# A graph layer's edge sums: a block's sums loaded in 6 transfers of 4 runs instead of 3 of 12, attributes by 8 groups, 15 instead of 13 groups of rows on SyncE

## The chip, the cores and the metric

One core of a Trainium2 chip runs the kernel. The metric is the device time of one execution in microseconds (us), less is better. The median of three runs stands for a kernel.

## The reference

12500 nodes with 160 features each (64 scalars and 32 vectors of 3), 412500 edges sorted by their destination:

```python
h = relu(layernorm(x))
l0, l1 = h[:, :64] @ W_l1_0, h1 @ W_l1_1            # per node; h1: 32 vectors of 3
w = relu(edge_attr_10 @ W_fc1 * a) * b @ W_fc2      # per edge, 192 weights
y0, y1 = l0[src], l1[src]                           # a gather of 160 numbers per edge
m0, m1, m2, m3 = products of w, y0, y1, edge_attr_4 # per edge
s0..s3 = segment_sum(m0..m3, dst)                   # per node, 4 x 160 numbers
out = x + a_node * (h @ W_si + 0.5 * (s @ W_l2))    # per node
```

## The kernel before, in words

**Setup.** x is loaded by 14 pieces; per block of 128 nodes the layer norm's statistics, the transposes and the products with W_l1 are made, and the rows of l (160 numbers, 640 B) are written to the table T (`l_table`) in DRAM, four blocks at a time (L555). Meanwhile POOL gathers the raw x of 21 groups of edges, which SP stores in `raw_rows` (L547). ACT's queue loads the index tables: `bas` and `dsti` (1.6 MB each, into the space of R) in round q = 8 of 25, `src` (1.6 MB) in round 14. On DVE the function `test` compares them in pieces from round 11 on; its flag decides whether the main stage may run.

**Main stage.** The edges are 806 groups of 512 (4 tiles of 128). For each group PE makes the radial layer (L1189) and the 192 weights per edge (L1199), DVE multiplies them with the gathered rows (`weigh`, L1113 and L1116), PE sums a tile's products over windows of 8 nodes with a matrix of positions (`sums`, L1212), DVE moves the sums to E (L1100, 4 buffers), and SP stores E in DRAM as `s_tiles` (B), one store for two groups (L903).

The rows of l that a group needs come in four ways. POOL gathers them from T, four indirect DMAs per group, up to 6 groups ahead (L867). 21 groups are computed again from `raw_rows`. 13 groups (`ROW`, spread evenly by `single`) are fetched by SP, one DMA for each of 512 rows (L930), of an address in a register; 32 addresses are loaded into registers at a time (L927). 14 groups (`ROWA`) are fetched the same way by ACT (L1038). `rows_at(g)` deals out the 512 rows of a group evenly over the groups between its predecessor and itself, in SP's program order, so that some 8 or 9 rows stand behind each group's store.

For each of 98 blocks of 128 nodes, once the edges that may hold it are summed (`due`, every 8 or 9 groups), SP loads 512 rows of B with `load_tiles` (L646), 4 rows per partition, into Z; DVE makes the matrix D of which row belongs to which node; PE adds them up with D (`place`, L682), LATE = 2 groups and more after that; ACT, PE and DVE then transpose, multiply with `pw` and add x, and SP stores the block (L738). A row of B has 8 x 160 numbers: four sums of 160, of which `place` needs all of the first (s0 and s3's part) and slices of the three others. `pieces_of` cuts the first 160 in three overlapping runs of 54, so that a block is three DMAs with 12 runs per partition each: 216, 256 and 128 B. Z's row is three slots of 150 numbers.

The edge attributes `ea` are loaded by four groups (L878, [112, 512], two buffers), `e4` by twelve (L884). Whatever SP does stands in one queue: `store`, `load_tiles`, `load_ea`, `store_rows`, `rows_at`, in this order for each g. The last two blocks are loaded in chunks (`load_chunk`, L625).

Of the kernel before, what the change touches and what calls it, by code (L numbers as in the profile page):

```python
# [7 lines left out]
C = 160  # L8
# [5 lines left out]
NROW = 13  # L14
# [4 lines left out]
SLOT = 150  # L19
# [71 lines left out]
def build(nc, a, n_nodes, n_edges):  # L91
# [16 lines left out]
    ZW = C + 3 * SLOT  # L108
# [25 lines left out]
    with ctx:  # L134
# [52 lines left out]
        ea = sb("ea", [112, 2, GE])  # L187
# [3 lines left out]
        ZP = 3 * SLOT  # L191
# [287 lines left out]

        def test():  # L480

            V.wait_ge(s_b, 48)
# [4 lines left out]
            V.wait_ge(s_d, 16)  # L487
# [12 lines left out]
            link(V.tensor_scalar(vio[:, 5:6], vio[:, 0:1], float(WIN - 1), None, ALU.is_gt))  # L500
            V.scalar_tensor_tensor(vio[:, 8:9], vio[:, 6:7], 0.0, vio[:, 5:6], ALU.is_lt, ALU.add).then_inc(s_fl, 1)
            yield

        def main_weights():
# [6 lines left out]
            V.wait_ge(s_b, 48)  # L511
# [101 lines left out]
        def pieces_of(z, o, n):  # L613

            def rows(at, step, width):
                return bass.AP(tensor=B.tensor, offset=o + at, ap=[[8 * C, n], [step, 3], [1, width]])

            return ((z[:, :, 96:SLOT], rows(0, 53, SLOT - 96)), (z[:, :, 0:64], rows(3 * C, 2 * C, 64)),
                    (z[:, :, 64:96], rows(3 * C + 64, 2 * C + 32, 32)))

        def load_chunk(e, c, part):
            o = ((ends[L] - SPAN) * WIN + 128 * c) * 8 * C
            z = Z[:, L % 2, c, :].rearrange("p (k c) -> p k c", c=SLOT)
            to, of = pieces_of(z, o, 128)[part]
            e.dma_start(to, of).then_inc(s_zc[c], 16)  # L625
# [47 lines left out]
        def place(j, g):  # L673
# [3 lines left out]
            PE.wait_ge(s_z[j % 2], 48 * (j // 2 + 1))  # L677
# [127 lines left out]
        with nc.If(way == 0):  # L805
# [22 lines left out]
            s_rw = [sem(f"s_rw{i}") for i in range(len(ROW))]  # L828
            s_rwa = [sem(f"s_rwa{i}") for i in range(len(ROWA))]
# [84 lines left out]
            def row(i, n):  # L914
# [15 lines left out]
                SP.dma_start(lone[i % 2][p:p + 1, t, :].bitcast(u8), TB[:, bass.ds(v, 4 * C)]).then_inc(s_rw[i], 16)  # L930
# [19 lines left out]
            for g in range(NG):  # L950
# [8 lines left out]
                if g % 4 == 1:  # L959
                    load_ea(g // 4 + 2)  # L960
# [62 lines left out]
            def act_row(i, n):  # L1023
# [14 lines left out]
                AC.dma_start(lone_act[p:p + 1, i % 2, t, :].bitcast(u8), TB[:, bass.ds(v, 4 * C)]).then_inc(s_rwa[i], 16)  # L1038
# [111 lines left out]
            for g in range(NG):  # L1150
                V.wait_ge(s_wp, g + 1)
                for u in pairs(g):
# [27 lines left out]
            def radial(p):  # L1180
                if 2 * p >= NG:
                    return
                q = p // 2
                PE.wait_ge(s_ea[q % 2], 16 * (q // 2 + 1))
                for i in range(min(2, NG - 2 * p)):
# [3 lines left out]
                    m = PE.matmul(bank[i][0:100, 0:GE], w1s[o:o + 10, :], ea[o:o + 10, q % 2, :], start=True, stop=True)  # L1189
# [96 lines left out]
        with nc.Else():  # L1286
# [14 lines left out]
            row = sb("row", [128, 128], i32)  # L1301
            tri = sb("tri", [128, 128])
            sel = sb("sel", [128, 128])
            low = sb("low", [128, 128])
            one = sb("one", [128, 2], i32)
            ef = sb("ef", [128, 4])
            df = sb("df", [128, 3])
            ix = sb("ix", [128, 2, 4], i32)
# [7 lines left out]
            SP.dma_start(tri[:, :], a["tri"]).then_inc(f_0, 16)  # L1316
# [3 lines left out]
            with nc.Fori(0, NG * G) as i:  # L1320
# [13 lines left out]
                PE.matmul(bank[0][0:100, 0:128], w1s[0:10, :], ea[0:10, 0, 0:128], start=True, stop=True).then_inc(f_pe, 1)  # L1334
# [42 lines left out]
                for q in range(2):  # L1377
                    PE.matmul(bank[4 + q][:, 0:2 * C], sel[:, :], M[:, 2 * q:2 * q + 2, :], start=True,
# [19 lines left out]
def lay_out(v, n_nodes, n_edges):  # L1398
# [18 lines left out]
    NR = -(-NG // 4)  # L1417
# [34 lines left out]
    for d in range(3):  # L1452
        n = 53 if d < 2 else 54
        r = C + SLOT * d + 96
        pw[r:r + n] = zero[53 * d:53 * d + n]
# [71 lines left out]
```

## Time and profile before

| | |
|---|---|
| median of 3 runs | 3937.83 us (3935.28 to 3940.37) |
| the profiled execution | 3939.58 us, of it the span of the trace 3935.8 us |
| granted clock of TensorE | 0.863 of full speed |
| busy: PE, DVE, ACT, POOL | 83%, 60%, 19%, 75% of the span |
| DMA | 827774 packets, 589.86 MB |

The page's engines are PE (matrix products), DVE, ACT and POOL; SP (SyncE) has no arithmetic and is all queue. A "q" behind an engine's name marks its sequencer: an instruction that issues a DMA is busy there and not in the engine's busy time. In the timeline a row is one instruction, or several alike in a row (x8), with start and duration in us. The gather on POOL is an instruction of its own and does count as busy.

### The profile page before, as it was taken

How to read it: one execution, taken by the hardware profiler on the slowest of the kernel's cores; microseconds unless marked ns; L12 is line 12 of the kernel's file. 1: busy time of each engine (PE TensorE's matmuls, PEld its weight loads, DVE VectorE, ACT ScalarE, POOL GpSimd, SP SyncE). 2: the span in 40 equal slices, each digit the busy share in tenths (PEclk: the TensorE clock that was granted, in tenths of full speed). 3: DMA queues.
4: the chain of work that ended last, by engine and by line, in shares of the span. 5: the costliest groups of instructions: out<-in, count | busy, mean ns of one | idle time of the engine just before them, and what ended most of it. 6: DMA issues, size and time to landing. Idle time of an engine off the chain costs nothing.

```text
span 3935.8 us, 83918 instructions
## 1 busy us (share of the span) xinstructions
PE 3247.8 (83%) x17464; PEld 1918.8 (49%) x17464; DVE 2363.2 (60%) x8236; ACT 748.3 (19%) x1681; POOL 2947.5 (75%) x3119
## 2 busy tenths in 40 slices
PE   5788788888888877887888887988888888888887
PEld 4454444454444444444554444545454455555444
DVE  7455556565665656565666556556666566666655
ACT  5111112111111111111121212111112121211111
POOL 6777777777777777777777777777777777777776
PEclk8788889888998889788898889788888888989788
DMA  9565656565556565656566565656656565656655
GB/s 316 151 145 134 149 140 147 143 149 140 146 147 148 143 146 143 147 141 149 140 156 147 146 153 139 151 140 153 147 144 150 142 150 145 148 145 148 150 145 134
DMA packets 827774, 589.86 MB, mean 150 GB/s; under 512 B 535130, under 2 KB 748654, under 8 KB 826878
## 3 DMA queue, kind: packets, MB, share of 16 engines
q1 hardware_dynamic: 660752, 317.60, 31.0%
q0 software_dynamic: 149520, 255.42, 27.6%
q10 hardware_dynamic: 16990, 11.41, 1.1%
q8 instruction: 151, 2.47, 0.3%
q14 instruction: 361, 2.96, 0.2%
HBM read 429.06 MB, written 155.04 MB: 148 GB/s over the span
## 4 chain that ended last, share of the span: by engine, by line
PE 20%; SPq 18%; ACTq 16%; issue 15%; POOL 15%; DMA 10%; DVE 6%; ACT 2%; DVEq 0%; POOLq 0%
POOL R L867 13%; ACTq L1038 11%; SPq L930 10%; DMA R<-l_table,src 6%; PE bank L682 6%; PE bank L1199 6%; ACTq L1035 4%; PE bank L1212 3%; PE bank L1189 3%; DMA s_tiles<-E 3%; SPq L927 3%; DVE R L1116 3%; SPq L646 3%; PE bank L725 1%; DVE R L1113 1%
## 5 line engine op out<-in xcount | busy, mean ns | idle before, releaser
L867 POOL DMA_INDIRECT R<-l_table,src x3031 | 2865.7, 945 | 934.8 <-issue 843.3
L1199 PE MATMUL bank<-w,hs 100*128 100x192 f32 x6446 | 1388.0, 363 | 97.7 <-ACT hs L979 77.4
L1199 PEld LDWEIGHTS bank<-w,hs 100*128 100x128 f32 x6446 | 1181.3, 212 | 416.8 <-issue 286.0
L1113 DVE TENSOR_TENSOR R<-bank,R 128x256 f32<-128x256 f32 x1558 | 654.2, 420 | 1129.6 <-PE bank L1199 786.8
L1116 DVE TENSOR_TENSOR R<-bank,R 128x192 f32<-128x192 f32 x3116 | 954.2, 348 | 0.0
L1212 PE MATMUL bank<-R 128*32 128x320 f32 x6448 | 679.0, 495 | 307.1 <-DVE R L1116 300.3
L979 ACT ACTIVATE hs<-bank 100x512 f32<-100x512 f32 x806 | 437.4, 594 | 2159.1 <-PE bank L1189 991.3
L1100 DVE COPY E<-bank 128x320 f32<-128x320 f32 x806 | 391.8, 486 | 230.9 <-DMA s_tiles<-E 179.7
L1189 PE MATMUL bank<-ea,w1s 10*100 10x512 f32 x1612 | 515.0, 718 | 10.7 <-DMA ea<-in_ea_p 9.9
L682 PE MATMUL bank<-ZD 128*128 128x450 f32 x776 | 413.6, 688 | 100.2 <-issue 96.8
L1212 PEld LDWEIGHTS bank<-R 128*32 128x32 f32 x6448 | 143.8, 113 | 528.7 <-issue 411.7
L682 PEld LDWEIGHTS bank<-ZD 128*128 128x128 f32 x776 | 179.3, 243 | 349.9 <-issue 343.2
L1090 DVE TENSOR_TENSOR R<-bank,e 128x128 f32<-128x128 f32 x806 | 235.1, 292 | 27.4
L1189 PEld LDWEIGHTS bank<-ea,w1s 10*100 10x100 f32 x1612 | 113.2, 177 | 256.6 <-issue 245.4
L725 PE MATMUL bank<-pw,zt 128*128 128x160 f32 (+1 forms) x970 | 195.6, 359 | 49.2 <-ACT zt L719 44.2
L725 PEld LDWEIGHTS bank<-pw,zt 128*128 128x128 f32 (+1 forms) x970 | 167.9, 229 | 128.3 <-ACT zt L719 71.8
L1087 DVE TENSOR_TENSOR bank<-bank,rel 128x32 f32<-128x32 f32 x806 | 153.2, 190 | 0.0
L687 ACT ACTIVATE zz<-bank 128x450 f32<-128x450 f32 x98 | 53.6, 547 | 399.1 <-PE bank L682 380.4
L733 DVE SCALAR_TENSOR_TENSOR os<-bank,av,x 128x160 f32<-128x160 f32 x98 | 37.4, 382 | 117.4 <-PE bank L725 114.9
L296 POOL DMA_INDIRECT ZD<-in_xa,src_raw x84 | 81.7, 972 | 34.8 <-issue 25.0
L711 ACT ACTIVATE zt<-bank 128x512 f32<-128x512 f32 x97 | 58.1, 599 | 173.8 <-issue 114.6
L693 ACT ACTIVATE zz<-x,nb,rs 128x160 f32<-128x160 f32 x98 | 51.0, 521 | 137.0 <-issue 118.7
(114 smaller groups left out, 898.2 us busy)
## 6 DMA issues: line engine op xcount, KB each, us to landing
s_tiles<-E SPq DMA_DIRECT2D x395, 320.0 KB
lone_act<-l_table ACTq DMA_DIRECT2D x7168, 0.6 KB
psc<-l_table SPq DMA_DIRECT2D x3584, 0.6 KB
H<-l_table SPq DMA_DIRECT2D x3072, 0.6 KB
R<-l_table,src POOLq DMA_INDIRECT x3031
ea<-in_ea_p SPq DMA_DIRECT2D x202, 224.0 KB
ZD<-s_tiles SPq DMA_DIRECT2D x97, 384.0 KB
ZD<-s_tiles SPq DMA_DIRECT2D x97, 324.0 KB
```

What stands on the lines that cost most here:

```text
L682: m = PE.matmul(bank[7][:, 0:ZP], D[:, j % 2, c, :], Z[:, j % 2, c, :], start=c == 0, stop=c == NCH - 1)
L725: m = PE.matmul(home(j, placed)[:, 0:C], turned(j, placed, q)[0:n, :], pw[0:n, q, :], start=q == 0, stop=q == 4)
L867: PL.indirect_dma_start(out=Y[:, g % NB, t, :], out_offset=None, in_=T, in_offset=bass.IndirectOffsetOnAxis(ap=src[:, k:k + 1], axis=0),). ...
L930: SP.dma_start(lone[i % 2][p:p + 1, t, :].bitcast(u8), TB[:, bass.ds(v, 4 * C)]).then_inc(s_rw[i], 16)
L979: AC.activation(hs[:, g % 4, :], bank[g % 2][0:100, 0:GE], ACT.Relu, scale=REL).then_inc(s_hs, 1)
L1038: AC.dma_start(lone_act[p:p + 1, i % 2, t, :].bitcast(u8), TB[:, bass.ds(v, 4 * C)]).then_inc(s_rwa[i], 16)
L1100: V.tensor_copy(E[:, g % 4, :], bank[5 + g % 2][:, 0:2 * C]).then_inc(s_e, 1)
L1113: V.tensor_tensor(p[:, :, :, 0:64], w[:, :, 0:128].rearrange("p t (s c) -> p t s c", s=2), y[:, :, 0:64].unsqueeze(2).to_broadcast([128, n ...
L1116: m = V.tensor_tensor(p[:, :, s, 64:160].rearrange("p t (d c) -> p t d c", d=3), w[:, :, 128 + 32 * s:160 + 32 * s].unsqueeze(2).to_broadc ...
L1189: m = PE.matmul(bank[i][0:100, 0:GE], w1s[o:o + 10, :], ea[o:o + 10, q % 2, :], start=True, stop=True)
L1199: m = PE.matmul(b[:, o * 192:(o + 1) * 192], hs[:, g % 4, t * 128:(t + 1) * 128], w2[:, :], start=True, stop=True, skip_group_check=True)
L1212: m = PE.matmul(b[q, 0:2 * C], S[:, g % 2, t, :], P[:, g % 2, t, :], start=True, stop=True)
```

## The change

Three things are changed on SP and one in the setup.

A block's sums: the slots are 96 numbers instead of 150, and the first 160 numbers of a row are loaded whole, in a run of 640 B. The load is six DMAs with 4 runs per partition each (640, 384, 256, 128, 256, 128 B). The attributes are loaded by eight groups, with a layout in DRAM that keeps a partition's 4 KB together. SP fetches the rows of 15 groups instead of 13. The index tables are loaded in rounds 12, 14 and 18 instead of 8, 8 and 14, and the test's pieces run from round 15 on. The semaphores of the row buffers are shared by eight groups; the path of the flag that isn't taken uses D's space for its own tiles.

```diff
-NROW = 13
+NROW = 15
-SLOT = 150
+SLOT = 96
...
-    ZW = C + 3 * SLOT
+    ZW = 2 * C + 3 * SLOT
...
-        ea = sb("ea", [112, 2, GE])
+        ea = sb("ea", [112, 2, 2, GE])
...
-        ZP = 3 * SLOT
+        ZP = C + 3 * SLOT
...
+            if q == min(12, NQ - 1):
                 AC.dma_start(bas[:, :, :], a["bases"].rearrange("o (g t) -> o g t", t=G).to_broadcast([128, NG, G])
-                             ).then_inc(s_b, 16)
+                             ).then_inc(s_d, 16)
+            if q == min(14, NQ - 1):
                 AC.dma_start(dsti[:, :, :], a["dst_t"].rearrange("p (g t) -> p g t", t=G)).then_inc(s_d, 16)
-            if q == min(14, NQ - 1):
+            if q == min(18, NQ - 1):
                 AC.dma_start(src[:, :], a["src_t"]).then_inc(s_i, 16)
...
-            if q >= 11:
+            for _ in range(0 if q < 15 else 1 if q % 2 else 2):
                 next(pieces, None)
...
             r0 = (ends[j] - SPAN if ends[j] > SPAN else 0) * WIN
-            z = Z[:, j % 2, :, :].rearrange("p n (k c) -> p (n k) c", c=SLOT)
-            for to, of in pieces_of(z, r0 * 8 * C, 128 * NCH):
-                SP.dma_start(to, of).then_inc(s_z[j % 2], 16)
+            every = B[r0 * 8 * C:(r0 + 128 * NCH) * 8 * C].rearrange("(p c x) -> p c x", p=128, x=8 * C)
+            z = Z[:, j % 2, :, :]
+            SP.dma_start(z[:, :, 0:C], every[:, :, 0:C]).then_inc(s_z[j % 2], 16)
+            SP.dma_start(z[:, :, C:C + 96], every[:, :, 3 * C:3 * C + 96]).then_inc(s_z[j % 2], 16)
+            for k in (1, 2):
+                to, of = C + SLOT * k, (2 * k + 3) * C
+                SP.dma_start(z[:, :, to:to + 64], every[:, :, of:of + 64]).then_inc(s_z[j % 2], 16)
+                SP.dma_start(z[:, :, to + 64:to + 96], every[:, :, of + 64 + 32 * k:of + 96 + 32 * k]).then_inc(s_z[j % 2], 16)
...
-            PE.wait_ge(s_z[j % 2], 48 * (j // 2 + 1))
+            PE.wait_ge(s_z[j % 2], 96 * (j // 2 + 1))
...
-                if 4 * q >= NG:
+                if 8 * q >= NG:
                     return
                 if q >= 2:
-                    SP.wait_ge(s_h, 2 * q - 2)
-                SP.dma_start(ea[:, q % 2, :], a["ea_p"][q, :, :]).then_inc(s_ea[q % 2], 16)
+                    SP.wait_ge(s_h, 4 * q - 4)
+                SP.dma_start(ea[:, q % 2, :, :], a["ea_p"][:, 2 * q:2 * q + 2, :]).then_inc(s_ea[q % 2], 16)
...
-                if g % 4 == 1:
-                    load_ea(g // 4 + 2)
+                if g % 8 == 5:
+                    load_ea(g // 8 + 2)
```

## Rows read from the trace of the kernel before

**Rows 1.** The page: span, busy time of the engines, the chain that ended last.

```profile
span 3935.8 us, 83918 instructions
...
PE 3247.8 (83%) x17464; PEld 1918.8 (49%) x17464; DVE 2363.2 (60%) x8236; ACT 748.3 (19%) x1681; POOL 2947.5 (75%) x3119
...
PE 20%; SPq 18%; ACTq 16%; issue 15%; POOL 15%; DMA 10%; DVE 6%; ACT 2%; DVEq 0%; POOLq 0%
```

**Rows 2.** Waits of SP, 400 to 3700 us: us in total, times, longest.

```profile
SPq L903 <- DVE E L1100: 26.9, 42, 3.1
SPq L642 <- DMA s_tiles<-E: 15.4, 18, 2.4
SPq L927 <- DVE R L1116: 12.0, 8, 2.7
```

**Rows 3.** Groups of instructions, 400 to 3700 us: count, busy us, mean ns, idle before.

```profile
L867 POOL DMA_INDIRECT R<-l_table,src x2631 | 2487.5, 945 | 812.8 <-issue 731.7 <-DVE R L1116 81.1
...
L1100 DVE COPY E<-bank 128x320 f32<-128x320 f32 x702 | 341.4, 486 | 216.4 <-DMA s_tiles<-E 171.6 <-PE bank L1212 29.0 <-issue 0.8
```

**Rows 4.** SP's issues by line, 400 to 3700 us: ns minimum/median/maximum.

```profile
L930 SPq DMA_DIRECT2D H<-l_table x3072: 227/228/2052, 422.4 to 3551.7; - x192
...
L930 SPq DMA_DIRECT2D psc<-l_table x2854: 227/228/2185, 403.6 to 3699.7; - x191
...
L927 SPq TENSOR_LOAD <-src_row x185: 2037/2215/2849, 405.5 to 3677.9; - x185
...
L903 SPq DMA_DIRECT2D s_tiles<-E x352: 387/393/771, 408.8 to 3697.9; - x176
...
L646 SPq DMA_DIRECT2D ZD<-s_tiles x256: 595/877/4305, 399.2 to 3689.8; - x128
...
L878 SPq DMA_DIRECT2D ea<-in_ea_p x176: 334/458/1921, 409.3 to 3684.2; - x176
...
L738 SPq DMA_DIRECT2D out<-os x86: 377/468/2673, 401.0 to 3684.7; - x86
```

**Rows 5.** Timeline of SP, from 1053 us: start, duration, instruction.

```profile
1053.22 5.20 SPq L930 DMA_DIRECT2D H<-l_table  x16
1058.51 0.39 SPq L903 DMA_DIRECT2D s_tiles<-E  x1
1061.79 4.16 SPq L930 DMA_DIRECT2D H<-l_table  x13
```

**Rows 6.** Timeline of SP at two blocks' loads.

```profile
1035.81 3.39 SPq L646 DMA_DIRECT2D ZD<-s_tiles  x3
1039.31 3.71 SPq L930 DMA_DIRECT2D H<-l_table  x8
...
1071.35 4.59 SPq L646 DMA_DIRECT2D ZD<-s_tiles  x3
1076.05 3.92 SPq L930 DMA_DIRECT2D H<-l_table  x8
```

**Rows 7.** Timeline of SP in the setup, third and fourth load of x.

```profile
2.27 0.57 SPq L265 DMA_DIRECT2D x<-in_xp  x1
...
2.89 3.20 SPq L265 DMA_DIRECT2D x<-in_xp  x1
```

**Rows 8.** Issues of L555 and L625, whole span, and a timeline row of six.

```profile
L555 SPq DMA_DIRECT2D l_table<-ls x25: 372/373/2241, 22.9 to 107.6; - x25
...
L625 SPq DMA_DIRECT2D ZD<-s_tiles x11: 370/482/1791, 3899.6 to 3923.8; - x11
...
3899.61 4.45 SPq L625 DMA_DIRECT2D ZD<-s_tiles  x6
```

**Rows 9.** Timelines of ACT's queue, SP and POOL in the setup.

```profile
40.45 0.49 ACTq L471 DMA_DIRECT2D R<-in_bases  x1
...
40.91 13.40 SPq L547 DMA_DIRECT2D raw_rows<-ZD  x1
...
60.32 0.95 POOL L296 DMA_INDIRECT ZD<-in_xa,src_raw  x1 [7.10 <-DMA raw_rows<-ZD]
```

More of the change, by code:

```diff
@@ L480, in test @@
         def test():
-            V.wait_ge(s_b, 48)
+            V.wait_ge(s_b, 32)
             V.tensor_tensor(gap[:, 0, :], bound[:, 0, :], bound[:, 1, :], ALU.subtract)
@@ L486, in test @@
             yield
-            V.wait_ge(s_d, 16)
+            V.wait_ge(s_d, 32)
             for q in range(NCUT):
@@ L510, in main_weights @@
             V.tensor_scalar(src_act[:, :, :], src_act[:, :, :], 4.0 * C, None, ALU.mult).then_inc(s_by, 1)
-            V.wait_ge(s_b, 48)
+            V.wait_ge(s_b, 32)
             last = 1 if side_by_side(n_nodes, n_edges) else 0
@@ L611, in turned @@
             return zt[:, q, :]
[L613 to L619, printed above, removed]
         def load_chunk(e, c, part):
             o = ((ends[L] - SPAN) * WIN + 128 * c) * 8 * C
-            z = Z[:, L % 2, c, :].rearrange("p (k c) -> p k c", c=SLOT)
-            to, of = pieces_of(z, o, 128)[part]
-            e.dma_start(to, of).then_inc(s_zc[c], 16)
+            z = Z[:, L % 2, c, C:ZP].rearrange("p (k c) -> p k c", c=SLOT)
+            r = B[o:o + 128 * 8 * C].rearrange("(p k c) -> p k c", k=4, c=2 * C)
+            d = B[o + 3 * C + 64:o + 3 * C + 64 + 128 * 8 * C].rearrange("(p x) -> p x", x=8 * C)[:, 0:3 * (2 * C + 32)]
+            if part == 0:
+                e.dma_start(Z[:, L % 2, c, 0:C], r[:, 0, 0:C]).then_inc(s_zc[c], 16)
+            if part == 1:
+                e.dma_start(z[:, :, 0:64], r[:, 1:4, C:C + 64]).then_inc(s_zc[c], 16)
+            if part == 2:
+                e.dma_start(z[:, :, 64:96], d.rearrange("p (k c) -> p k c", k=3)[:, :, 0:32]).then_inc(s_zc[c], 16)
         def place_chunk(c):
@@ L652, in load_nodes @@
                 SP.wait_ge(s_t5, j - 1)
-            y = z[:, C:ZW].rearrange("p (k c) -> p k c", c=SLOT)
-            SP.dma_start(y[:, :, 96:SLOT], bass.AP(tensor=A.tensor, offset=j * 128 * 4 * C, ap=[[4 * C, 128], [53, 3], [1, 54]])
-                         ).then_inc(s_z[j % 2], 16)
+            y = z[:, 2 * C:ZW].rearrange("p (k c) -> p k c", c=SLOT)
+            SP.dma_start(z[:, C:2 * C], r[:, 0, :]).then_inc(s_z[j % 2], 16)
             SP.dma_start(y[:, :, 0:64], r[:, 1:4, 0:64]).then_inc(s_z[j % 2], 16)
@@ L827, in build @@
             s_rp = sem("s_rp")
-            s_rw = [sem(f"s_rw{i}") for i in range(len(ROW))]
-            s_rwa = [sem(f"s_rwa{i}") for i in range(len(ROWA))]
+            s_rw = [sem(f"s_rw{i}") for i in range(8)]
+            s_rwa = [sem(f"s_rwa{i}") for i in range(8)]
             lone = [psc[:, :, :].rearrange("p q c -> p (q c)")[:, 0:G * C].rearrange("p (t c) -> p t c", t=G),
@@ L929, in row @@
                 v = bass.RuntimeValue.of_register_unchecked(held_sp[n % RB]).with_bounds(min_val=0, max_val=(NP - 1) * 4 * C)
-                SP.dma_start(lone[i % 2][p:p + 1, t, :].bitcast(u8), TB[:, bass.ds(v, 4 * C)]).then_inc(s_rw[i], 16)
+                SP.dma_start(lone[i % 2][p:p + 1, t, :].bitcast(u8), TB[:, bass.ds(v, 4 * C)]).then_inc(s_rw[i % 8], 16)
                 SP.free_register(held_sp[n % RB])
@@ L1037, in act_row @@
                 v = bass.RuntimeValue.of_register_unchecked(held[n % RA]).with_bounds(min_val=0, max_val=(NP - 1) * 4 * C)
-                AC.dma_start(lone_act[p:p + 1, i % 2, t, :].bitcast(u8), TB[:, bass.ds(v, 4 * C)]).then_inc(s_rwa[i], 16)
+                AC.dma_start(lone_act[p:p + 1, i % 2, t, :].bitcast(u8), TB[:, bass.ds(v, 4 * C)]).then_inc(s_rwa[i % 8], 16)
                 AC.free_register(held[n % RA])
@@ L1162, in build @@
                     elif g in row_of:
-                        V.wait_ge(s_rw[row_of[g]], 16 * GE)
+                        V.wait_ge(s_rw[row_of[g] % 8], 16 * GE * (row_of[g] // 8 + 1))
                     elif g in rowa_of:
-                        V.wait_ge(s_rwa[rowa_of[g]], 16 * GE)
+                        V.wait_ge(s_rwa[rowa_of[g] % 8], 16 * GE * (rowa_of[g] // 8 + 1))
                     else:
@@ L1182, in radial @@
                     return
-                q = p // 2
+                q, h = p // 4, p // 2 % 2
                 PE.wait_ge(s_ea[q % 2], 16 * (q // 2 + 1))
@@ L1188, in radial @@
                     o = 64 * (p % 2) + 32 * i
-                    m = PE.matmul(bank[i][0:100, 0:GE], w1s[o:o + 10, :], ea[o:o + 10, q % 2, :], start=True, stop=True)
+                    m = PE.matmul(bank[i][0:100, 0:GE], w1s[o:o + 10, :], ea[o:o + 10, q % 2, h, :], start=True, stop=True)
                 m.then_inc(s_h, 1)
@@ L1300, in build @@
             BIG = float(1 << 22)
[L1301 to L1308, printed above, removed]
+            row = D[:, 0, 0, :].bitcast(i32)
+            tri = D[:, 0, 1, :]
+            sel = D[:, 0, 2, :]
+            low = D[:, 0, 3, :]
+            one = D[:, 1, 0, 0:2].bitcast(i32)
+            ef = D[:, 1, 1, 0:4]
+            df = D[:, 1, 2, 0:3]
+            ix = D[:, 1, 3, 0:8].bitcast(i32).rearrange("p (b k) -> p b k", b=2)
             M = Y[:, 1, 0:4, :]
@@ L1315, in build @@
                          flat_zt[:, 0:4 * C].unsqueeze(1).to_broadcast([128, NT, 4 * C])).then_inc(f_0, 16)
-            SP.dma_start(tri[:, :], a["tri"]).then_inc(f_0, 16)
+            SP.dma_start(tri, a["tri"]).then_inc(f_0, 16)
             for e in (PL, V):
@@ L1324, in build @@
                 four = nc.snap(i * 64 + 64, min_val=64, max_val=NG * G * 64)
-                SP.dma_start(ea[0:10, 0, 0:128], a["ea_t"][:, bass.ds(e0, 128)]).then_inc(f_ld, 16)
+                SP.dma_start(ea[0:10, 0, 0, 0:128], a["ea_t"][:, bass.ds(e0, 128)]).then_inc(f_ld, 16)
                 SP.dma_start(one[:, 0:1], a["src_f"][bass.ds(e0, 128), :]).then_inc(f_ld, 16)
                 SP.dma_start(one[:, 1:2], a["dst_f"][bass.ds(e0, 128), :]).then_inc(f_ld, 16)
-                SP.dma_start(row[:, :], a["dst_r"][:, bass.ds(e0, 128)].to_broadcast([128, 128])).then_inc(f_ld, 16)
-                SP.dma_start(ef[:, :], a["e4_f"][bass.ds(e0, 128), :]).then_inc(f_ld, 16)
+                SP.dma_start(row, a["dst_r"][:, bass.ds(e0, 128)].to_broadcast([128, 128])).then_inc(f_ld, 16)
+                SP.dma_start(ef, a["e4_f"][bass.ds(e0, 128), :]).then_inc(f_ld, 16)
                 for e in (PE, PL, V):
@@ L1333, in build @@
                                       in_offset=bass.IndirectOffsetOnAxis(ap=one[:, 0:1], axis=0)).then_inc(f_g, 16)
-                PE.matmul(bank[0][0:100, 0:128], w1s[0:10, :], ea[0:10, 0, 0:128], start=True, stop=True).then_inc(f_pe, 1)
+                PE.matmul(bank[0][0:100, 0:128], w1s[0:10, :], ea[0:10, 0, 0, 0:128], start=True, stop=True).then_inc(f_pe, 1)
                 AC.wait_ge(f_pe, 1)
@@ L1347, in build @@
                 flink(V.tensor_copy(df[:, 0:1], one[:, 1:2]))
-                flink(V.tensor_scalar(sel[:, :], row[:, :], df[:, 0:1], None, ALU.is_equal))
-                flink(V.tensor_tensor(low[:, :], sel[:, :], tri[:, :], ALU.mult))
-                flink(V.tensor_reduce(df[:, 1:2], low[:, :], AX.X, ALU.max))
+                flink(V.tensor_scalar(sel, row, df[:, 0:1], None, ALU.is_equal))
+                flink(V.tensor_tensor(low, sel, tri, ALU.mult))
+                flink(V.tensor_reduce(df[:, 1:2], low, AX.X, ALU.max))
                 flink(V.tensor_scalar(df[:, 2:3], df[:, 1:2], BIG, None, ALU.mult))
@@ L1377, in build @@
                 for q in range(2):
-                    PE.matmul(bank[4 + q][:, 0:2 * C], sel[:, :], M[:, 2 * q:2 * q + 2, :], start=True,
+                    PE.matmul(bank[4 + q][:, 0:2 * C], sel, M[:, 2 * q:2 * q + 2, :], start=True,
                               stop=True).then_inc(f_pe, 1)
@@ L1416, in lay_out @@
     w1s = np.zeros((112, 100), f)
-    NR = -(-NG // 4)
+    NR = -(-NG // 8) * 2
     both = np.zeros((10, NR * 4 * GE), f)
@@ L1420, in lay_out @@
     both = both.reshape(10, NR, 4, GE).transpose(1, 2, 0, 3)
-    ea_p = np.zeros((NR, 112, GE), f)
+    ea_p = np.zeros((112, NR, GE), f)
     for r in range(4):
         w1s[32 * r:32 * r + 10] = v["L0_gnn_W_fc1"]
-        ea_p[:, 32 * r:32 * r + 10] = both[:, r]
+        ea_p[32 * r:32 * r + 10] = both[:, r].transpose(1, 0, 2)
     one = np.zeros((C, C), f)
@@ L1441, in lay_out @@
     pw[0:64, 0:64] = v["L0_gnn_W_si0"]
-    zero = np.zeros((C, C), f)
-    zero[0:64, 0:64] = v["L0_gnn_W_l2_00"]
+    pw[160:224, 0:64] = v["L0_gnn_W_l2_00"]
     for d in range(3):
@@ L1446, in lay_out @@
         pw[64 + 32 * d:96 + 32 * d, q] = v["L0_gnn_W_si1"]
-        zero[q, q] = v["L0_gnn_W_l2_11"]
-        r = C + SLOT * d
+        pw[224 + 32 * d:256 + 32 * d, q] = v["L0_gnn_W_l2_11"]
+        r = 2 * C + SLOT * d
         pw[r:r + 64, q] = v["L0_gnn_W_l2_01"]
@@ L1451, in lay_out @@
         psc[r + 64:r + 96] = k / np.sqrt(3.0)
[L1452 to L1455, printed above, removed]
     fold = lambda m: np.ascontiguousarray(m.reshape(5, 128, C).transpose(1, 0, 2))
```

## The prediction

> **What bounds the kernel now.** The first part of the page [rows 1] shows PE busy for 83% of the span, POOL for 75%, DVE for 60%, and its chain of waits divides itself between PE, SyncE's queue (18%), ACT's queue and POOL: no engine stands out, so busy shares don't answer the question. I take the steady part of the main stage, 400 to 3700 us, and ask each sequence of instructions how long it stood still.
>
> In that stretch DVE evacuated 702 groups [rows 3], so a group takes 3300 / 702 = 4.70 us. POOL made 2631 gathers of 945 ns, with 812.8 us between them, of which 731.7 us is issue time (about 0.305 us each) [rows 3]. 2631 x 1.25 us = 3289 us of 3300: POOL never rests. The reader is to see there that a busy share of 75% is a full engine. What takes 4 gathers away from POOL is worth 4 x 1.25 = 5.0 us, if nothing else is full.
>
> But SyncE (SP) is full too. It waited 26.9 + 15.4 + 12.0 us in the three largest rows [rows 2]; with the smaller ones I take 60 us. It works for 3240 of 3300 us, 98%. This can be added up from counts [rows 4] and prices. A row issue of L930: 16 in 5.20 us and 13 in 4.16 us [rows 5], the last one counted with its 0.23 us alone, is 0.33 us each with the register move; the load of 32 addresses (L927) is 2.2 us by its median [rows 4] and 0.09 us of gaps, 2.3 us. A store of E is 0.39 + 0.05 us, a load of attributes 0.46 + 0.05, an output store 0.47 + 0.05. So: 5926 rows x 0.33 = 1956; 185 loads x 2.3 = 426; 352 stores x 0.44 = 155; 176 x 0.51 = 90; 86 x 0.52 = 45.
>
> The last item is the block's sums (L646), and its price is larger than its own rows say. Three issues take 3.39 us in one block and 4.59 us in another, and what follows is late as well: the 8 rows behind them take 3.71 and 3.92 us [rows 6], where 7 x 0.33 + 0.23 = 2.54 us is usual. With 0.1 us of gap the two blocks cost 4.66 and 6.07 us; I take 5.4 us. 85 blocks x 5.4 = 459 us. The sum is 3131 us of the 3240, the rest (109 us) being the loads of e4 and of raw rows and small irregularities. The budget closes within 4%, and SP has next to nothing to give.
>
> **The change part by part.**
>
> Rows: two more groups are fetched by SP, 1024 rows. 1024 x 0.33 + 32 x 2.3 = +412 us of SP. POOL loses 8 gathers, 8 x 1.25 = -10 us. No DVE, PE or ACT instruction is added; a weighing from the row buffer costs what one from Y costs. The groups stand 52 to 55 apart instead of 58 to 64, and the first one at 52 instead of 60, so its 512 rows go out in 46 groups.
>
> Attributes: half as many issues of the same 112 partitions, each twice as long. 101 x 0.51 = -52 us of SP. They are asked for two buffers ahead, so that a longer landing is hidden behind at least 6 groups (28 us).
>
> A block's sums: 36 runs per partition in 3 issues become 24 runs in 6, 4608 runs against 3072 for the 128 partitions; bytes are nearly the same (7200 and 7168 per partition). Why does the present load cost 5.4 us? The first issue of 1536 runs takes about 0.6 us (its minimum in [rows 4] is 595 ns), and the maximum there is 4305 ns: something fills up and the queue holds SP back. The loads of x in the setup give its size from another side: each is 896 runs; the third was taken in 0.57 us and the fourth took 3.20 us [rows 7]. So 2688 runs are taken without a stall, and 3584 are not. The new load has 3072 in all, spread over six issues' time, in which the first ones drain. Without a stall an issue of 512 runs is that of L555, 373 ns [rows 8], and for one right behind another the chunk loads of L625 (384 runs) have a median of 482 ns [rows 8]. 0.39 + 5 x 0.48 + 6 x 0.05 = 3.1 us. Call the cost of a block X. The bounds: from below, six at L555's price with gaps, 2.5 us; from above, the stall stays whole, 5.4 us. The nearest row is the run of six L625 issues in 4.45 us [rows 8], one of which stalled (1791 ns at most). I take 3.1, because one stall in eleven such issues is rare. The 94 blocks that are loaded while rows are being issued save 94 x (5.4 - 3.1) = -216 us.
>
> The cheapest issue of the trace, a row's single run of 640 B, takes 227 ns, and the store of E takes at least 387 [rows 4]. The Trainium skill (DMA: Bandwidth & Descriptors, "Anatomy of one DMA") puts the sequencer's dispatch of a DMA at about 50 ns and calls descriptor generation small. The trace does not agree; an estimate by that page would be 0.3 us for six issues, and SP would have room to spare.
>
> The layout: the product of a block is 448 columns instead of 450, the last transpose 96 rows instead of 98: nothing. The weights' rows are moved with it. The loads are wanted only from LATE on (two groups and more), so that six landings are as good as three.
>
> The setup: `bas`, `dsti` and `src` go out one at a time and later. In the trace the first two are issued at 40.4 us back to back, SP's next store of raw rows then takes 13.40 us, and POOL stands for 7.10 us, its only long wait before the main stage [rows 9]. POOL runs from there into the main stage without a pause. If the three loads fit between others the 7 us go; each is still 1.6 MB, so I take -6 us, with 0 and -7 as ends. The pieces of the test on DVE are dealt out over later rounds and end in the last one, as before.
>
> **The sum.** SP: +412 - 52 - 216 = +144 us of work. SP's present idle time (60 us in 3300, some 65 in the whole stage) absorbs what it can; the waits for a landed store (15.4 us, [rows 2]) stay, so about 55 can be used. That leaves +89 us. SP takes the place of POOL as the engine that sets the pace. Whoever is late next: the store of E waits in SP's queue behind rows, DVE waits for its buffer (already 171.6 us of L1100's idle time [rows 3]), then PE for DVE, and POOL for its Y buffers. POOL's 10 us are lost in it. With the setup's -6: +83 us. The profiled execution took 3939.6 us (3935.8 of span and 3.8 around it), which is 1.8 us above the median of the runs; 3939.6 + 83 = 4023, less 1.8 and with the tail after the last row untouched: 4020 us. In general the time is about 3729 + 94 X.
>
> **The rivals.**
>
> SP becomes the bound and the stall goes (the forecast): X from 2.5 to 4.45 us gives 3964 to 4147. For it: the 98% and the additive budget. Against: the budget has 109 us that I can't name. Chance 0.56.
>
> The stall stays: the DMA engines drain the runs at their own pace, and six issues wait for it as three did. X = 4.45 to 5.4 and over, 4147 to 4237. For it: the row behind the three issues is late too, so what fills up is not emptied by pausing; the present blocks cost 4.7 to 6.1 us. Against: the x loads' 2688 runs. Chance 0.24. The Trainium skill (the same page, "Specifications") says that below 512 B a transfer is short of line rate; of the 24 new runs only 4 are longer, so by it the engines' time falls little, which speaks for this rival. The two blocks of [rows 6] can't tell that from a limit on the number of runs.
>
> The other side: POOL stays the bound. It decides at X = 2.1 us: 3729 + 94 x 2.1 = 3926, which is where POOL's own time lies, 3938 - 10 - 6 = 3922. Faster by 0.4%. For it: the row issues could lose part of their unexplained 109 us once the queue is no longer choked, worth another 1 us of X; then 2.5 to 3 would do. Or an issue of 512 runs costs only what a row's issue does, 0.23 us [rows 4]: then X is 6 x 0.23 + 0.3 = 1.7 us, 3729 + 160 = 3889, and POOL's 3922 decides. The page's rule on dispatch, weighed above, would lead to this as well. Against: 512 runs took 372 ns at the least [rows 8], so that six are 2.5 us, and a trade of 412 us against 268 can't come out even. Chance 0.14 (0.02 of it for the cheap issue). Between this case and the forecast, X of 2.1 to 2.3 us, the time stays within 0.2% of now: 0.06.
>
> **How the numbers follow.** A measurement of this kernel tells 0.2% (8 us) from no change. Faster 0.14, within 0.2% 0.06, slower 0.80. The time is the first case's, 4020, with its own range 3964 to 4147. The range for 8 in 10 reaches down to POOL's case at 3924 and up to 4150, into the case of the stall that stays; some 0.06 is left out below and 0.14 above.
>
> **What would show it.** In the profile after: group time of about 4.8 us in the steady stretch; SP's waits for DVE (L903) near zero; POOL's idle time released by DVE no longer 81 us but several tens of us more; DVE's idle time at L1100 by the landing of the store of E well over 171.6 us; the issues of a block near 0.4 to 0.5 us each with no issue over 2 us, and the 8 rows behind them in 2.5 us; no POOL wait of 7 us in the setup. The prediction is wrong if POOL's gathers still follow one another every 1.25 us, which would mean that a row or a block costs SP less than these rows say.

## The result: slower by 6%, SyncE sets the pace

The changed kernel took 4178.3 us in the median of 4 runs (4173 to 4184), the kernel before 3936.6 us beside it: ratio 1.061 (95% interval 1.059 to 1.064). The forecast was 4020 us, with a range up to 4150. The direction and the mechanism are as forecast; the loss is 242 us where 82 were forecast, nearly three times as much.

The page of the changed kernel, its span, its engines and the chain that ended last:

```profile
span 4180.0 us, 86178 instructions
PE 3314.1 (79%) x17464; PEld 1956.0 (47%) x17464; DVE 2357.8 (56%) x8236; ACT 746.8 (18%) x1681; POOL 2939.8 (70%) x3111
...
SPq 53%; issue 15%; PE 12%; DMA 7%; ACTq 7%; DVE 4%; POOL 1%; ACT 1%; DVEq 0%; POOLq 0%
SPq L934 32%; SPq L931 9%; ACTq L1042 5%; DMA s_tiles<-E 5%; PE bank L1203 3%; PE bank L686 3%; SPq L651 3%; SPq L650 2%; SPq L907 2%; PE bank L1216 2%; PE bank L1193 2%; ACTq L1039 2%; DVE R L1120 1%; SPq L647 1%; SPq L742 1%
```

SP's queue had 18% of the chain in [rows 1] and has 53% now; its rows (L934) and the loads of their addresses (L931) alone make 41%. The reader is to see also what doesn't show it: the busy shares of PE, DVE, ACT and POOL have all fallen by 1 to 5 points, since all wait, and SP has no busy share at all.

Who waited for whom, SP's own waits and two groups of DVE and POOL, 400 to 3900 us of the changed kernel (as [rows 2, 3], in a stretch 200 us longer):

```profile
SPq L642 <- DMA s_tiles<-E: 20.5, 19, 2.7
...
SPq L907 <- DVE E L1104: 5.0, 18, 0.4
SPq L931 <- DVE R L1120: 4.9, 6, 1.3
```

```profile
L1104 DVE COPY E<-bank 128x320 f32<-128x320 f32 x696 | 339.9, 488 | 486.8 <-DMA s_tiles<-E 424.3 <-PE bank L1216 39.2 <-issue 5.7
...
L871 POOL DMA_INDIRECT R<-l_table,src x2606 | 2463.6, 945 | 1036.7 <-issue 698.3 <-DVE R L1120 338.4
```

A group takes 3500 / 696 = 5.03 us instead of 4.70. SP waits for DVE's sums 5.0 us in all where it waited 26.9 [rows 2]. DVE waits 424.3 us for the store of E where it waited 171.6, and POOL 338.4 us for the Y buffers where it was 81.1 [rows 3]: the chain of followers that the prediction named.

A block's load in the timeline of SP, changed kernel, two blocks (as [rows 6]):

```profile
1007.36 0.53 SPq L646 DMA_DIRECT2D ZD<-s_tiles  x1
1007.94 0.62 SPq L647 DMA_DIRECT2D ZD<-s_tiles  x1
1008.62 0.66 SPq L650 DMA_DIRECT2D ZD<-s_tiles  x1
1009.32 0.64 SPq L651 DMA_DIRECT2D ZD<-s_tiles  x1
1010.00 0.63 SPq L650 DMA_DIRECT2D ZD<-s_tiles  x1
1010.67 1.47 SPq L651 DMA_DIRECT2D ZD<-s_tiles  x1
1012.24 5.66 SPq L934 DMA_DIRECT2D H<-l_table  x10
...
1049.95 0.53 SPq L646 DMA_DIRECT2D ZD<-s_tiles  x1
...
1053.34 0.66 SPq L651 DMA_DIRECT2D ZD<-s_tiles  x1
1054.10 3.32 SPq L934 DMA_DIRECT2D H<-l_table  x10
```

From the first issue to the first row 4.88 and 4.15 us; the ten rows behind are 0.1 to 0.2 us over their usual time (9 x 0.33 + 0.23 = 3.2, and 2.3 for the register load that the first ten contain). So these two blocks cost SP 5.0 and 4.3 us. Read in the same way, all 85 blocks between 400 and 3900 us take 4.77 us on average from the first issue to the next instruction, and what follows is 0.3 us late: 5.1 us a block. The forecast had 3.1. The last issue took over 1 us in 47 of the 85. The 85 blocks of the kernel before, 400 to 3700 us, cost 5.7 us (4.39 and 1.3) where the prediction took 5.4 from two of them. The issues of these lines over the whole span, ns minimum/median/maximum:

```profile
L650 SPq DMA_DIRECT2D ZD<-s_tiles x194: 518/649/2089, 209.6 to 4158.8; - x194
...
L651 SPq DMA_DIRECT2D ZD<-s_tiles x194: 518/677/1922, 210.2 to 4159.4; - x194
```

**A measure for SP.** What a kernel asks of SP is the stretch less SP's waits, by group. It is 4.61 us before (3300 less the 62 us of all its waits, 702 groups) and 4.97 for the changed kernel (3500 less 39.6, 696 groups). POOL needs 4.67 to 4.69, its gathers per group in the stretch at 1.25 us each. SP's number is used below. A stall at an issue is counted in it as work, and it comes from one execution of each kernel.

### The profile page after: what moved, and what is told of

Same layout as the page of the kernel before. It is cut to its first block, busy times and chain, and to the rows that moved or that the text cites. A ratio compares the mean times of both kernels' runs of the same rounds, so it can differ in the third digit from the quotient of the medians.

```text
span 4180.0 us, 86178 instructions
## 1 busy us (share of the span) xinstructions
PE 3314.1 (79%) x17464; PEld 1956.0 (47%) x17464; DVE 2357.8 (56%) x8236; ACT 746.8 (18%) x1681; POOL 2939.8 (70%) x3111
## 4 chain that ended last, share of the span: by engine, by line
SPq 53%; issue 15%; PE 12%; DMA 7%; ACTq 7%; DVE 4%; POOL 1%; ACT 1%; DVEq 0%; POOLq 0%
SPq L934 32%; SPq L931 9%; ACTq L1042 5%; DMA s_tiles<-E 5%; PE bank L1203 3%; PE bank L686 3%; SPq L651 3%; SPq L650 2%; SPq L907 2%; PE bank L1216 2%; PE bank L1193 2%; ACTq L1039 2%; DVE R L1120 1%; SPq L647 1%; SPq L742 1%
## 5 line engine op out<-in xcount | busy, mean ns | idle before, releaser
L1203 PEld LDWEIGHTS bank<-w,hs 100*128 100x128 f32 x6446 | 1203.3, 215 | 416.4 <-issue 283.1
L686 PE MATMUL bank<-ZD 128*128 128x448 f32 x776 | 459.3, 754 | 232.9 <-issue 219.7
L1193 PE MATMUL bank<-ea,w1s 10*100 10x512 f32 x1612 | 524.1, 730 | 14.0 <-DMA ea<-in_ea_p 13.2
L686 PEld LDWEIGHTS bank<-ZD 128*128 128x128 f32 x776 | 199.4, 270 | 507.1 <-issue 488.6
L729 PE MATMUL bank<-pw,zt 128*128 128x160 f32 (+1 forms) x970 | 186.7, 348 | 51.0 <-ACT zt L723 45.9
L691 ACT ACTIVATE zz<-bank 128x448 f32<-128x448 f32 x98 | 53.2, 543 | 594.1 <-PE bank L686 584.2
L709 PEld LDWEIGHTS bank<-ident,zz 128*128 128x128 f32 x392 | 44.4, 149 | 69.9 <-issue 69.0
```

Source lines behind the costliest of these rows:

```text
L686: m = PE.matmul(bank[7][:, 0:ZP], D[:, j % 2, c, :], Z[:, j % 2, c, :], start=c == 0, stop=c == NCH - 1)
L729: m = PE.matmul(home(j, placed)[:, 0:C], turned(j, placed, q)[0:n, :], pw[0:n, q, :], start=q == 0, stop=q == 4)
L1203: m = PE.matmul(b[:, o * 192:(o + 1) * 192], hs[:, g % 4, t * 128:(t + 1) * 128], w2[:, :], start=True, stop=True, skip_group_check=True)
```

## The experiments

Of 18 runs, 6 (f and i, on two chips) were beside a kernel before of 3936 or 3937 us. The 12 others (e, g, h, j) ran on three other chips, where the kernel before took 5526 to 5613 us at a granted clock near 0.71; the last section has what is known of that. Their ratios are given, but the arithmetic of the prediction is tried on f and i.

| run | groups of rows | a block's load | before there, us | ratio (95%) | SP's work per group, us |
|---|---|---|---|---|---|
| changed | 15 | 6 close together | 3936.6 | 1.061 (1.059 to 1.064) | 4.97 |
| f1 | 13 | 6 close together | 3936.2 | 0.998 (0.997 to 0.999) | 4.46 |
| f2 | 15 | 3 close together, all else as before | 3936.2 | 1.084 (1.082 to 1.086) | 5.09 |
| f3 | 15 | 6, both sides of one shape | 3936.2 | 1.057 (1.055 to 1.059) | 4.95 |
| f4 | 15 | 6 between rows | 3936.2 | 1.056 (1.054 to 1.057) | 4.90 |
| i1 | 15 | 3 between rows | 3936.7 | 1.053 (1.051 to 1.055) | 4.89 |
| i2 | 14 | 3 between rows | 3936.7 | 1.020 (1.016 to 1.023) | 4.67 |
| e1 | 13 | as f1 | 5606.9 | 0.994 (0.991 to 0.998) | |
| e2 | 15 | as f2 | 5606.9 | 1.047 (1.043 to 1.051) | |
| e3 | 13 | 6, attributes and index tables loaded as before | 5606.9 | 0.998 (0.997 to 1.000) | |
| e4 | 15 | as f3 | 5606.9 | 1.031 (1.027 to 1.035) | |
| g1, h1 | 15 | as i1 | 5525.8, 5530.4 | 1.037, 1.038 (each within 0.004) | |
| g3, h2 | 14 | as i2 | 5525.8, 5530.4 | 1.013, 1.014 (each within 0.004) | |
| g4, h3, j1 | 15 | 3 of the 6 | 5525.8, 5530.4, 5613.4 | 1.019, 1.021, 1.019 | |
| j2 | 14 | 6 close together | 5613.4 | 1.015 (1.011 to 1.019) | |

**Rows alone: e1, f1, e2, f2, e3.** Theory A: SP's queue is the bound and the rows filled it. Its rival B: the six loads land late and hold the sums up.

```diff
-NROW = 15
+NROW = 13
```

> The changed kernel with the rows of 13 groups on SP instead of 15; six loads, attributes by eight groups and the later index tables stay. Theory A (SP's queue sets the pace; the two groups of rows are what it can't carry): 1024 rows x 0.41 us = 418 us of work leave SP, which then needs about 3762 us where POOL needs 3930, so POOL's gathers set the pace again: 3925 to 3945 us, ratio 0.997 to 1.002. Theory B (the six loads of a block land later or hold the matrix sums up, and the rows are harmless): little changes, above 4100 us.

> The same kernel as e1_rows13 once more, because there the kernel before itself took 5607 us with a granted clock of 0.70. Theory A: POOL's gathers follow one another every 1.25 us, 3925 to 3945 us where the kernel before takes 3938. Theory B: above 4100.

f1 took 3927.3 us, 9 us less than before; in e1 the ratio was 0.994. With the same six loads and 13 groups nothing is slow, so B falls. f2 is the kernel before with `NROW = 15` alone:

> The kernel before with the rows of 15 groups on SP and nothing else of the change. Theory A: 3938 + 418 of row work - 50 of SP's idle time that is used up = 4300 us (4270 to 4330), slower than the changed kernel's 4178 by what six loads and the attributes save. Theory B: the rows cost nothing, 3925 to 3945 us.

> The same kernel as e2_before_rows15 once more, where the kernel before takes 3938. Theory A: 4270 to 4330 us. Theory B: 3925 to 3945.

4267.4 us: the rows alone cost 331 us, and the time is 3 us under the expected range. The rest of the change gives back 89 of them. e3 has the six loads with 13 groups, and of the rest of the change only the shared semaphores, the flag's other path and the attributes' layout in DRAM:

> The kernel before with a block's sums in six loads (and the layout that belongs to them), 13 groups of rows, attributes by four groups, index tables where they were. Theory A: SP gets freer by 50 to 70 us of work and POOL sets the pace as before: 3930 to 3945 us. Theory B: above 4100 us.

0.998 (0.997 to 1.000), on a slower chip only: no measurable cost, and hardly a gain. f1's groups and SP's largest waits, 400 to 3700 us (as [rows 2, 3]):

```profile
L871 POOL DMA_INDIRECT R<-l_table,src x2638 | 2493.9, 945 | 807.2 <-issue 738.1 <-DVE R L1120 69.1
...
L1104 DVE COPY E<-bank 128x320 f32<-128x320 f32 x704 | 341.3, 485 | 90.9 <-DMA s_tiles<-E 55.6 <-PE bank L1216 22.9 <-issue 1.4
```

```profile
SPq L907 <- DVE E L1104: 105.3, 65, 6.5
SPq L642 <- DMA s_tiles<-E: 23.1, 22, 2.6
SPq L931 <- DVE R L1120: 15.9, 10, 2.6
```

POOL makes 2638 gathers in 3300 us, one per 1.251 us, and SP waits 160.7 us in all (105.3 of them for DVE). What the change frees on SP is what SP now stands idle: POOL can't use it.

**An issue's price by its shapes: e4, f3.** In the changed kernel the DRAM side of a transfer is 512 rows with one stride and the SBUF side 128 partitions of 4. With another assignment of rows both sides are (128, 4, width). A partition then takes rows 128 apart instead of 4 neighbours, so that the order of the addresses changes with the shapes.

```diff
-... .rearrange("(p c x) -> p c x", p=128, x=8 * C)
+... .rearrange("(c p x) -> p c x", p=128, x=8 * C)
```

> The changed kernel, but partition p of a block's load takes rows p, 128 + p, 256 + p, 384 + p of the sums instead of rows 4p to 4p + 3, so that both sides of each transfer have the same three dimensions (128, 4, width); the matrix of positions follows. Runs, bytes and issues are the same. Theory P (an issue's price depends on the shapes: 0.65 us now against 0.48 us for the chunk loads, whose two sides match): six issues get cheaper by about 1 us, 94 blocks, about 4085 us. Theory Q (an issue behind another costs 0.65 us and the last one waits for room whatever the shapes): 4170 to 4190 us.

> The same kernel as e4_mapped once more. In e4_mapped an issue of a block's load had medians of 0.39 us for the first and 0.50 for the others, against 0.53 and 0.63 in e1_rows13. Six issues are then 0.75 us cheaper, 94 blocks, 70 us of SP: 4178 - 70 = 4110 us (4090 to 4125). If SP's queue weren't the bound, or if room in the queue and not the issue set the price, it would stay at 4170 to 4190.

f3 took 4159.7 us, 19 us less than the changed kernel's 4178.3, where 70 were expected. Its timeline shows why:

```profile
1003.52 1.43 SPq L650 DMA_DIRECT2D ZD<-s_tiles  x1
1004.99 1.63 SPq L651 DMA_DIRECT2D ZD<-s_tiles  x1
...
1044.61 0.40 SPq L646 DMA_DIRECT2D ZD<-s_tiles  x1
1045.06 0.55 SPq L647 DMA_DIRECT2D ZD<-s_tiles  x1
1045.66 0.49 SPq L650 DMA_DIRECT2D ZD<-s_tiles  x1
1046.19 0.51 SPq L651 DMA_DIRECT2D ZD<-s_tiles  x1
1046.74 0.51 SPq L650 DMA_DIRECT2D ZD<-s_tiles  x1
1047.30 0.92 SPq L651 DMA_DIRECT2D ZD<-s_tiles  x1
1048.32 3.23 SPq L934 DMA_DIRECT2D H<-l_table  x10
```

The first four issues are each 0.1 to 0.2 us cheaper than in the changed kernel's blocks, as theory P has it, and the last ones take much of it back: 0.92 us here, 1.43 and 1.63 in the block before. Over all 85 blocks between 400 and 3900 us the last issue took more than 1 us in 68, where it was 47 of 85 in the changed kernel, and a block costs 4.9 us instead of 5.1; 94 x 0.2 = 19 us is what the time fell by. Issues that come faster stall more often at the end. P holds for the price and fails for the time.

**Issues apart from one another: f4.** One issue, then one after every second row of the same group.

```diff
+                            if n % 2 == 0:
+                                load_part()
```

> The changed kernel with the six issues of a block's load put between the rows of the same group (one, then one after every second row) instead of one behind another. Runs, bytes and order are the same. Theory Q (an issue close behind another large one costs more, 0.65 against 0.53, and the last ones and the next instruction wait for room, 1.1 us a block): 5 x 0.12 + 1.1 = 1.7 us a block, 94 blocks, 4178 - 160 = 4020 us (3990 to 4060). Theory P (the price belongs to the shapes and the stalls to the number of runs, wherever they stand): 4160 to 4190.

f4 took 4151.2 us, 27 us less where 160 were expected. Its timeline of SP:

```profile
1083.94 0.52 SPq L658 DMA_DIRECT2D ZD<-s_tiles  x1
1084.57 0.74 SPq L941 DMA_DIRECT2D H<-l_table  x2
1085.36 0.52 SPq L658 DMA_DIRECT2D ZD<-s_tiles  x1
1085.98 0.43 SPq L941 DMA_DIRECT2D H<-l_table  x1
1086.46 0.52 SPq L658 DMA_DIRECT2D ZD<-s_tiles  x1
1087.08 0.57 SPq L914 DMA_DIRECT2D s_tiles<-E  x1
```

An issue takes 0.52 us, and the stalls are gone: the longest of 582 took 0.96 us. But whatever stands behind one is dearer: a row 0.43 instead of 0.23 us, two rows 0.74 instead of 0.56, a store of E 0.57 instead of 0.39; over the stretch of 400 to 3900 us it is 0.19 us on average. An issue of 512 runs costs 0.52 + 0.1 + 0.2 = 0.8 us in its place, six of them 4.9. The sum for Q had counted the stall and forgotten this.

**Three issues between rows: g1, h1, i1; with 14 groups: g3, h2, i2.** After f4 theory S was a price per issue, and its rival D the time in which the DMA engines drain the runs. The old load of three issues is put between the rows:

```diff
+                            if m % 4 == 0:
+                                load_part()
```

> The changed kernel with the old load of a block (three issues of 12 runs per partition, slots of 150 numbers), these three put between the rows of the same group (one, then one after every fourth row); 15 groups of rows, attributes by eight groups, later index tables. Theory S (what a block costs SP is a price per issue: in f4_spread each of six took 0.53 us, 0.08 of gaps and 0.19 more in the row behind it; three of 0.60 + 0.08 + 0.19 are 2.6 us against 5.1): 4178 - 94 x 2.5 = 3943 us (3925 to 3970). Theory D (the queue gives room no faster than the DMA engines drain the runs, about 5 us a block, so that what is saved in one place comes back in another, as in f3_mapped and f4_spread): with 4608 instead of 3072 runs no better than 4150, up to 4230.

> The same kernel as g1_three_spread15 once more, because there the kernel before took 5526 us with a granted clock of 0.71 and each row of SP cost 0.56 us where it costs 0.35 otherwise. In g1 an issue between rows had medians of 0.60, 0.59 and 0.57 us and the row behind it took 0.49 on average (0.26 more than usual): 3 x (0.59 + 0.08 + 0.26) = 2.8 us a block against 5.1. Theory S, where the kernel before takes 3938: 4178 - 94 x 2.3 = 3962 us (3945 to 3980). Theory D: 4150 to 4230.

> The kernel of g1 and h1 a third time, for a chip on which the kernel before takes 3938. Theory S: 3962 us (3945 to 3980). Theory D: 4150 to 4230.

i1 took 4148.0 us, 2 us under D's range. S is refuted: half the issues bring 3 us against f4, which is within the spread of the executions. D isn't shown by it: 4608 runs took no longer than f4's 3072. SP's timeline in i1, with issues of 1536 runs:

```profile
1007.36 0.59 SPq L655 DMA_DIRECT2D ZD<-s_tiles  x1
1008.05 2.07 SPq L939 DMA_DIRECT2D H<-l_table  x4
1010.17 0.59 SPq L655 DMA_DIRECT2D ZD<-s_tiles  x1
1010.85 1.94 SPq L939 DMA_DIRECT2D H<-l_table  x2
...
1046.76 0.59 SPq L655 DMA_DIRECT2D ZD<-s_tiles  x1
1047.44 1.63 SPq L939 DMA_DIRECT2D H<-l_table  x4
1049.12 0.59 SPq L655 DMA_DIRECT2D ZD<-s_tiles  x1
1049.80 1.15 SPq L939 DMA_DIRECT2D H<-l_table  x2
```

The issues are 0.59 us, and the rows behind them take 2.07, 1.94, 1.63 and 1.15 us where four take 1.22 and two 0.56: 0.85, 1.38, 0.41 and 0.59 us more, 0.8 on average. Over the stretch of 400 to 3900 us it is also 0.8. An issue of 1536 runs costs 0.59 + 0.1 + 0.8 = 1.5 us, three of them 4.5. Three issues more and 1536 runs less are worth about the same to SP here, which is why a load of six could not pay for 1024 rows.

> g1_three_spread15 with 14 groups of rows. Theory S: SP has 208 us less than in g1, so POOL sets the pace, with four gathers fewer than in f1_rows13: 3927 - 5 = 3922 us (3915 to 3930), faster than both kernels. Theory D: 3940 to 4020.

> The same kernel as g3_three_spread14 once more, where the kernel before takes 3938. Theory S: SP needs 3962 - 208 = 3754 us and POOL sets the pace: 3922 us (3915 to 3930). Theory D: 3940 to 4020.

> The kernel of g3 and h2 a third time, for a chip on which the kernel before takes 3938. Theory S: 3922 us (3915 to 3930). Theory D: 3940 to 4020.

i2 took 4015.4 us, in D's range. Its SP needs 4.67 us per group and POOL as much, but the pace was 3500 / 729 = 4.80, and SP waited 95 us of that stretch. The chain that ended last in i2 is PE 30%, ACT's queue 24%, SP's queue 13% and POOL 2%: neither SP nor POOL alone held it, and what PE and ACT's queue had to do with it was not tried.

**Half of the load left out: g4, h3, j1, and 14 groups as they are: j2.** g4, h3 and j1 leave three of a block's six issues out, so that parts of the sums aren't computed.

> The changed kernel without three of the six issues of a block's load (the last three: the second vector part's 32, the third's 64 and 32 numbers); their columns of the sums hold what an earlier block left, so that this part of the output isn't computed. 1536 instead of 3072 runs, still one behind another. Theory S: three issues at about 0.8 us less, 94 x 2.4 = 226: 3950 us (3935 to 3970). Theory D: the engines' time for the runs falls from 4.2 to 2.5 us by the packets' mean durations, 1.7 us a block: 4178 - 160 = 4018 (3990 to 4040).

> The same kernel as g4_three_of_six once more (three of the six issues of a block's load left out), where the kernel before takes 3938. Theory S: 3950 us (3935 to 3970). Theory D: 4018 us (3990 to 4040).

> The kernel of g4 and h3 (three of the six issues of a block's load left out, 1536 runs, one behind another; that part of the sums isn't computed) once more, for a chip on which the kernel before takes 3937. Theory M, formed after i1 and f4: on SP a large issue costs 0.42 us and 0.75 ns for each run, the instruction behind it included (512 runs: 0.53 + 0.08 + 0.19 = 0.80 us in f4; 1536 runs: 0.60 + 0.07 + 0.90 = 1.57 us in i1). Three issues of 512 runs less save 3 x 0.8 = 2.4 us or a little more with the stall of the last one, 94 x 2.5 = 235: 3943 us (3930 to 3965). Theory D (drain alone): 4018 (3990 to 4040).

> The changed kernel with 14 groups of rows on SP, nothing else different. SP's work is linear in the rows: 4178 - 512 x 0.41 = 3968 us if SP alone sets the time (3955 to 3985). If two queues that are both almost full cost extra, as i2 seems to show (SP waited 102 us there, and the time was 75 us over SP's line), 4000 to 4060. If POOL alone set it, 3922.

All four ran on the slower chips. There the load of half the runs is 0.9 to 1.2% under e4 (whose load has the other shapes; the changed kernel itself has no run there), and 14 groups are 1.5% over the kernel before where 13 are 0.6% under it. The order is that of theory A, but none of the numbers decides between M (a price for each issue and each run, in j1's expectation) and D, and the excess of i2 has no second measurement.

## Why the prediction was wrong

- *What bounds the kernel* was right. POOL without a pause and SP at 98% is what f1 and f2 confirm: two groups of rows on a queue with 60 us to spare cost 331 us.
- *Rows, +412 us of SP.* Between f1 and the changed kernel SP's work rises from 4.459 to 4.972 us per group, 806 x 0.513 = 413 us. Between the kernel before and f2 it is 4.613 to 5.087, 806 x 0.474 = 382 us.
- *A block's sums: the step that failed is the cost X of the six issues, "I take 3.1".* It measured 5.1 over the 85 blocks, and the old load 5.7 where 5.4 was taken, so that a block saves 0.6 us and not 2.3: 94 x 0.62 = 58 us of SP instead of 216. SP's work says the same. Before to f1, all of the change but the rows saves 806 x (4.613 - 4.459) = 124 us; less the 52 taken for the attributes 72 us are left, 0.8 per block; from f2 to the changed kernel it is 806 x (5.087 - 4.972) - 52 = 41 us, 0.4 per block. With 58 in the place of 216 the prediction's own sum gives 4020 + 158 = 4178 us, the measured time. That it hits so closely is luck: SP's waits were to give 55 us and gave 25 (806 x (62 / 702 - 39.6 / 696)), and other terms must have made up for that.
- Three things were wrong inside X. The 0.48 us of L625 come from transfers whose two sides have the same shape; here the shapes differ and the second to sixth issues have medians of 0.62 to 0.68 us (f3 brought them to 0.50 to 0.58). The loads of x were read as proof that 3072 runs find room; the last issue took over 1 us in 47 of 85 blocks. And nothing was set down for the instruction behind an issue, which f4 and i1 show to be 0.2 us late after 512 runs and 0.8 after 1536. The nearest row for six issues was in the prediction, 4.45 us [rows 8], and was argued away as a rare stall.
- *The rival "the stall stays"* described the time better (4147 to 4237) and named the reason only in part: f4 removed the stalls, and SP's work fell by 0.07 us per group, 57 us, the time by 27.
- *The rival that POOL stays the bound* fell: POOL's gathers came every 1.34 us and not every 1.25 (3500 / 2606). The reason given against it sets 412 us against 268; at the 2.5 us for six issues that it speaks of, the saving would be 94 x 2.9 + 52 = 325 us, which still doesn't come out even. The 50 ns of the Trainium skill for the dispatch (DMA: Bandwidth & Descriptors, "Anatomy of one DMA — SWDGE (gpsimd) path") stand there for a DMA that GpSimd issues, so they were no figure for SP's queue. No issue of a block took SP less than 0.518 us in the changed kernel.
- *The setup, -6 us.* POOL's one long wait fell from 7.10 us [rows 9] to 4.10:

```profile
72.17 0.94 POOL L296 DMA_INDIRECT ZD<-in_xa,src_raw  x1 [4.10 <-DMA raw_rows<-ZD]
```

  It moved from 60 us to 72 us and was 3 us shorter, not gone. In f1, where POOL sets the pace, it was 3.1 us. There the profiled executions are 13 us apart (3939.6 and 3926.2), the medians 9; beside the 4 us of this wait, POOL made 7 gathers more in the same 3300 us.
- *Attributes and layout* were not tried alone; nothing in the traces speaks against their terms. The attributes and the later tables together are what e1 has and e3 hasn't: 0.994 and 0.998 on one chip, a gain of about 0.5% there.
- What stays open: how much of a block's cost belongs to an issue and how much to a run. f4 and i1 give one price each (0.8 us for 512 runs, about 1.5 for 1536), which two constants always fit, and there is no third. What fills up when an issue stalls isn't shown. Why the time of i2 lies over the work of both queues is open as well.

## What to carry to other kernels

When the queue that only issues DMAs is full, add up its work as for an engine (the stretch less its waits, per iteration), and price a transfer by what stands from its first issue to the end of the next issue behind it, over many of them, not by the durations of its own rows and not by two examples. Fewer runs bought with more issues freed this queue little. And let a saving be measured before it is spent: the same change with 13 groups (f1) is a small gain over the kernel before, 0.2%, and the best version of this study; with 15 it costs 6%.

## What the runs showed of the hardware

In this kernel a DMA with more runs held SP longer, and partly in the next instruction: 0.23 us for one run, 0.39 for 256 [rows 4], 0.52 for 512 (f4) and 0.59 for 1536 (i1), with 0.2 us more in what follows 512 runs and 0.4 to 1.4 us in what follows 1536. The length of the runs made no difference: f4's six issues have runs of 128 to 640 B, and of all 582 the shortest took 523 ns, the median 524. The other assignment of rows did: the second issue of a block (L647) has a median of 0.50 us where both sides had the same three dimensions (f3) and 0.62 where they hadn't (the changed kernel). Whether that is the shapes or the order of the addresses was not separated.

The same program took 40% longer on some chips: 5526 to 5613 us on three (one of them twice, in e and j), 3936 and 3937 on two others. In e1 the span was 5555.4 us at a granted clock of 0.713. SP's rows were slow there, while the six issues of a block took what they take elsewhere, 0.53 us for the first and 0.64 for the last:

```profile
1501.96 8.15 SPq L934 DMA_DIRECT2D H<-l_table  x8
1510.22 0.53 SPq L646 DMA_DIRECT2D ZD<-s_tiles  x1
...
1513.50 0.64 SPq L651 DMA_DIRECT2D ZD<-s_tiles  x1
1514.24 8.04 SPq L934 DMA_DIRECT2D H<-l_table  x8
```

Eight rows take 8 us instead of 2.5, while the median of a row's issue is 228 ns as elsewhere: single instructions are held up for up to 1.4 us, and a register move, which takes 29 ns, does so too:

```profile
L934 SPq MOVE psc<-l_table x3584: 1/29/1419, 204.9 to 5444.4; - x200
L934 SPq DMA_DIRECT2D psc<-l_table x3584: 2/228/1414, 205.0 to 5444.4; - x200
```

On the usual chips a stall of the DMA queue doesn't reach the moves. In i1 a row's issue took up to 3.1 us and its move never more than 38 ns:

```profile
L939 SPq MOVE H<-l_table x3584: 29/29/38, 386.7 to 3807.5; - x200
L939 SPq DMA_DIRECT2D H<-l_table x3584: 224/228/3128, 386.7 to 3807.5; - x200
```

So what slows SP on the other chips is hardly the DMA queue. With rows that slow the last issue of a block took over 1 us in 1 of 90 blocks of e1 (400 to 5300 us), against 46 of 86 in f1 (400 to 3700 us), the same kernel. What holds the instructions up was not found. Each ratio in the table compares runs on one chip, but the balance between SP and POOL is another one on the slower chips, and so they answer another question.
